# Two group-normalized convolutions on one core: alternating rows, 32x64 products, one straight step on TensorE

## The chip, the cores and the metric

The kernel runs on one core of a Trainium2 chip. The time is device time in microseconds (us) for one execution. The core's engines are named as in the profile: PE is TensorE (PEld its loads of weights), DVE is VectorE, ACT is ScalarE, POOL is GpSimd, SP is SyncE, which only issues transfers (DMAs). Each runs its own program in order; they meet at semaphores. PSUM has eight banks of 128 partitions x 512 float32, into which TensorE alone adds up.

## The reference

```
def _gn(v, G=16, eps=1e-05):          # group norm: 16 groups of 2 channels
    ...
    return ((g - m) / jnp.sqrt(s + eps)).reshape(v.shape)

x = x + _L0_conv_ref(_gn(x), L0_conv_weight, L0_conv_threshold)   # 3x3, weights masked by a threshold
x = x + _L1_conv_ref(_gn(x), L1_conv_kernel, L1_conv_bias)        # 5x5, with bias
```

x has 16 images of 32 channels, 128 x 128, float32. Both convolutions keep the size. The second needs the mean and the variance of the whole image that the first has made.

## The kernel before, in words

**Tiling.** An image is worked in two halves, so there are 32 halves, h. The 128 partitions are four quads of 32 channels. For reading, quad i holds a band of rows with its halo (`x_bands`, 18 rows, six slots; `mid_bands`, 20 rows, three slots). For results, quad j of bank i holds the j-th part of band i: `mid` (five slots) and `x_own` (two slots) have four rows of 128 in each bank. A weight matrix of one tap is 32x32, so quad i of the image times tap t gives quad j of bank i for four rows: one product of 32 x 32 cells and 512 columns. 16 of them, for all i and j, are a set (`tap`, L784), and fill the array.

**Precision.** Image and weights are each the sum of two float16 values. A convolution is three passes: high image x high weights, high image x low weights, low image x high weights. The 3x3 has 9 sets per pass, the 5x5 25; together 102 sets per step.

**Steps.** Step s does the 3x3 convolution of half s and the 5x5 of half s - 3 (`LAG`). TensorE has a loop of bodies between which it branches (`first3`, `inner3`, `last3`, `first5`, `inner5`, `last5`, `low_image`, L796 to L861): the body of the 3x3 taps is run three times, with `s3` overwritten in between by ScalarE (`weights3`) and `x3` overwritten in place by VectorE with the low image (`low3`); the 5x5 body twice, with `s5` overwritten by ScalarE (`weights5`). Three lead steps have 3x3 alone, three last steps 5x5 alone.

**The other engines, in a step.** ScalarE empties the 5x5 banks (`take_conv5`), copies weights, takes roots, and writes the high images (`high3` for half s + 1, `high5` for half s - 2). VectorE writes the low images (`low5`, `low3`), normalizes in place (`normalize3`, `normalize5`, L597), makes `mid` from the 3x3 banks and `x_own` (`take_conv3`, which releases the banks through `bank3_go`), and takes statistics (`stats_in`, `stats_out`, `aggregate`). GpSimd adds the 5x5 result to `mid`. Once per image the statistics go over DRAM to all partitions (`spread_stats`, `gather_stats` on ScalarE's queue); VectorE sums them (`group_stats`), ScalarE takes the root, VectorE refines it (`scale_of`). In even steps from 4 to 28 there are two such statistics, one of `mid`, one of x.

**Transfers.** SyncE issues, in an order written out by hand: `load_bands`, `load_own`, `move_mid` (16 per half, from `mid` to `mid_bands`), `move_edges` (the rows that cross halves, 14 per image) and `store_out`.

Of the kernel before, what the change touches and what calls it, by code (L numbers as in the profile page):

```python
# [48 lines left out]
def two_blocks(nc, x, w3_dram, thr_dram, w5_dram, bias_dram, mix_dram, out):  # L49
# [7 lines left out]
    with ExitStack() as ctx:  # L57
# [14 lines left out]
        x3 = sbuf("x3", [P, R3, PITCH], F16)  # L72
# [18 lines left out]
        carrier = sbuf("carrier", [P, 2])  # L91
# [52 lines left out]
        c3_early = sem("c3_early")  # L144
        c3_inner = sem("c3_inner")
        c3_whole = sem("c3_whole")
        a5_inner = sem("a5_inner")
        a5_whole = sem("a5_whole")
        b5_whole = sem("b5_whole")
# [7 lines left out]

        hi5_done = sem("hi5_done")
        conv5_out = sem("conv5_out")
# [41 lines left out]
        MOVES = Q * Q + 2 * Q - 1  # L201
        CLEARED = 3 + XB_SLOTS + 2 * MB_SLOTS
# [4 lines left out]
        def own_rows(image, r, j):  # L207

            return image.rearrange("c (i r j a) w -> r j c i (a w)", i=BANKS, r=2, j=Q)[r, j]

        def band(r, i, halo):

            first = A * Q * (2 * i + r) - halo
# [9 lines left out]
        def _(sp):  # L223
            def load_own(h):
                for j in range(Q):
                    sp.dma_start(x_own[quad(j), h % X_SLOTS, :, :], own_rows(x[h // 2], h % 2, j),
                                 ).then_inc(x_own_in[h % X_SLOTS], 16)

            def store_out(k, banks):
                for j in range(Q):  # L230
                    sp.dma_start(own_rows(out[k // 2], k % 2, j)[:, banks, :], mid[quad(j), k % MID_SLOTS, banks, :],
                                 ).then_inc(out_stored[k % MID_SLOTS], 16)
# [7 lines left out]
            def move_rows(h, i, j, k, to, rows, at):  # L240

                sp.dma_start(mid_bands[quad(to), k % MB_SLOTS, at:at + rows.stop - rows.start, :],  # L242
                             mid[quad(j), h % MID_SLOTS, i, :].rearrange("p (a w) -> p a w", a=A)[:, rows, :],
                             ).then_inc(mid_bands_in[k % MB_SLOTS], 16)

            def move_mid(h):
                sp.wait_ge(mid_made, PIECES * (h + 1))
                for i in range(Q):
                    for j in range(Q):
                        move_rows(h, i, j, h, i, slice(0, A), 2 + A * j)  # L250

            def move_edges(n, source, to):

                sp.wait_ge(mid_made, PIECES * (2 * n + source + 1))
                for i in range(Q):
                    if source < to:
                        move_rows(2 * n, i, Q - 1, 2 * n + 1, i, slice(A - 2, A), 0)
                        if i:
                            move_rows(2 * n, i, 0, 2 * n + 1, i - 1, slice(0, 2), 2 + A * Q)
                    else:  # L260
                        move_rows(2 * n + 1, i, 0, 2 * n, i, slice(0, 2), 2 + A * Q)
                        if i + 1 < Q:
                            move_rows(2 * n + 1, i, Q - 1, 2 * n, i + 1, slice(A - 2, A), 0)
# [28 lines left out]
            for s in range(LAG, STEPS + 1):  # L292
# [10 lines left out]
                if has3(s + XB_SLOTS):  # L303
                    sp.wait_ge(norm1, s + 2)
# [12 lines left out]
        def _(pool):  # L317
            for t in (x3, x5_hi, x5_lo):
                nc.gpsimd.memset(t[:, :, 0:2], 0.0)
                nc.gpsimd.memset(t[:, :, PITCH - 2:PITCH], 0.0).then_inc(zeroed, 1)  # L320
            cleared = 3
# [18 lines left out]
            nc.gpsimd.tensor_copy(s5[:, :, :], s5_hi[:, :, :]).then_inc(w5_go, 1)  # L340
# [3 lines left out]
            for i in range(Q):  # L344
                for j in range(Q):
                    pool.dma_start(mid_bands[quad(i), 1, 2 + A * j:2 + A * (j + 1), :],
                                   mid[quad(j), 1, i, :].rearrange("p (a w) -> p a w", a=A),
                                   ).then_inc(mid1_moved, 16)
# [12 lines left out]
        def _(act):  # L361
# [6 lines left out]
            def high3(h):  # L368

                act.wait_ge(norm1, h + 1)  # L370
                if h:
                    act.wait_ge(c3_whole, 2 * h)
                nc.scalar.activation(x3[:, :, 2:2 + W], x_bands[:, h % XB_SLOTS, :, :], ACT.Copy).then_inc(x3_go, 2)  # L373

            def high5(k):

                act.wait_ge(norm2, k + 1)
                if k:
                    act.wait_ge(a5_whole, k)
                nc.scalar.activation(x5_hi[:, :, 2:2 + W], mid_bands[:, k % MB_SLOTS, :, :], ACT.Copy).then_inc(hi5_done, 1)  # L380

# [7 lines left out]

            def weights3(source, part, tokens):  # L390

                at, go = ((slice(0, 4), w3a_go), (slice(4, T3), w3b_go))[part]
                nc.scalar.activation(s3[:, at, :], source[:, at, :], ACT.Copy).then_inc(go, tokens)  # L393

            def weights5(source):
                nc.scalar.activation(s5[:, :, :], source[:, :, :], ACT.Copy).then_inc(w5_go, 1)  # L396
# [590 lines left out]
```

## Time and profile before

| | us |
|---|---|
| median of three runs | 855.02 (852.67 to 856.11) |
| the profiled execution | 854.08 |
| its span | 852.3 |
| TensorE busy (92%) | 780.7 |
| VectorE busy (81%) | 692.6 |
| ScalarE busy (38%) | 319.7 |
| GpSimd busy (38%) | 322.4 |
| mean TensorE clock | 0.983 of full |

The share of a busy engine is an average over stretches with different limits, so the rows further below take the span apart: by stretch, then one step, then the single instructions. In a row of the timeline the first number is the start in us from the span's start, the second the duration; `xN` is the number of instructions merged in it, and the bracket at its end is the idle time of that engine before it and what ended that. "issue" means that the profile shows nothing that was waited for.

### The profile page before, as it was taken

How to read it: one execution, taken by the hardware profiler on the slowest of the kernel's cores; microseconds unless marked ns; L12 is line 12 of the kernel's file. 1: busy time of each engine (PE TensorE's matmuls, PEld its weight loads, DVE VectorE, ACT ScalarE, POOL GpSimd, SP SyncE). 2: the span in 40 equal slices, each digit the busy share in tenths (PEclk: the TensorE clock that was granted, in tenths of full speed). 3: DMA queues.
4: the chain of work that ended last, by engine and by line, in shares of the span. 5: the costliest groups of instructions: out<-in, count | busy, mean ns of one | idle time of the engine just before them, and what ended most of it. 6: DMA issues, size and time to landing. Idle time of an engine off the chain costs nothing.

```text
span 852.3 us, 108960 instructions
## 1 busy us (share of the span) xinstructions
PE 780.7 (92%) x52277; PEld 694.1 (81%) x52277; DVE 692.6 (81%) x1008; ACT 319.7 (38%) x408; POOL 322.4 (38%) x164
## 2 busy tenths in 40 slices
PE   0874689999999999999999999999999999998995
PEld 0553579888989889889988989988998989987884
DVE  6877599899897989799898989899897968675432
ACT  0312134443443434443443434444343434443221
POOL 1035043333434443233444444333344444333331
PEclk9997799999999999999999999999999999999998
DMA  8999638788695968788685978878695737563413
GB/s 179 222 219 234 149 83 212 197 207 206 178 223 139 224 171 212 193 211 203 173 220 139 225 180 212 198 198 212 171 228 139 205 95 189 121 167 80 103 49 99
DMA packets 83778, 150.51 MB, mean 177 GB/s; under 512 B 21152, under 2 KB 28576, under 8 KB 79648
## 3 DMA queue, kind: packets, MB, share of 16 engines
q1 hardware_dynamic: 78624, 144.88, 69.0%
q10 hardware_dynamic: 4608, 4.23, 2.2%
q0 software_dynamic: 512, 1.05, 0.5%
q14 instruction: 25, 0.20, 0.1%
q8 instruction: 9, 0.15, 0.1%
HBM read 75.60 MB, written 33.59 MB: 128 GB/s over the span
## 4 chain that ended last, share of the span: by engine, by line
PE 78%; DVE 11%; issue 4%; DMA 3%; SPq 2%; DVEq 1%; ACT 1%; ACTq 0%; POOLq 0%; POOL 0%
PE psum L790 78%; DVE x L620 3%; SPq L242 2%; DMA mid_bands<-mid 1%; DMA x_bands<-x_dram 1%; DVE x_bands L605 1%; DVE bn_in L543 1%; DVEq L643 1%; DVE bn_out L648 1%; DVE mid_bands L605 1%; DVE mid L640 1%; DVE product L575 0%; DVE x_lo L628 0%; DVE deviation L579 0%; DVE gscale L594 0%
## 5 line engine op out<-in xcount | busy, mean ns | idle before, releaser
L354 POOL TENSOR_TENSOR mid<-mid,conv_out 128x512 f32<-128x512 f32 x122 | 300.4, 2492 | 471.9 <-ACT conv_out L387 471.9
L790 PE MATMUL psum<-x_hi,s 32*32 32x512 f16 x25600 | 373.1, 378 | 17.8 <-issue 10.3
L790 PEld LDWEIGHTS psum<-x_hi,s 32*32 32x32 f16 x25600 | 339.7, 88 | 42.1 <-issue 17.2
L790 PE MATMUL psum<-x,s 32*32 32x512 f16 x13824 | 225.3, 386 | 19.4 <-DVEq L643 12.0
L790 PEld LDWEIGHTS psum<-x,s 32*32 32x32 f16 x13824 | 174.8, 88 | 70.1 <-issue 40.1
L790 PE MATMUL psum<-x_lo,s_hi 32*32 32x512 f16 x12800 | 186.4, 376 | 3.2 <-issue 3.2
L790 PEld LDWEIGHTS psum<-x_lo,s_hi 32*32 32x32 f16 x12800 | 176.4, 88 | 8.3 <-issue 5.0
L628 DVE TENSOR_TENSOR x_lo<-mid_bands,x_hi 128x2560 f16<-128x2560 f32 x32 | 103.9, 3247 | 33.6 <-PE psum L790 31.6
L620 DVE TENSOR_TENSOR x<-x_bands,x 128x2304 f16<-128x2304 f32 x32 | 101.3, 3166 | 36.3 <-PE psum L790 36.3
L387 ACT ACTIVATE conv_out<-psum,bias,unscale 128x512 f32<-128x512 f32 x122 | 90.4, 769 | 61.1 <-PE psum L790 58.3
L396 ACT ACTIVATE s<-s_lo 128x800 f16<-128x800 f16 x29 | 25.3, 871 | 158.1 <-PE psum L790 158.1
L373 ACT ACTIVATE x<-x_bands 128x2304 f16<-128x2304 f32 x32 | 67.9, 2122 | 38.8 <-DVE x_bands L613 23.0
L640 DVE SCALAR_TENSOR_TENSOR mid<-psum,unscale,x_own 128x1024 f32<-128x1024 f32 x64 | 79.1, 1277 | 3.8 <-PE psum L790 2.8
L648 DVE BATCH_NORM_STATS2 bn_out<-mid 128x6 f32<-128x512 f32 x128 | 78.0, 668 | 2.2
L543 DVE BATCH_NORM_STATS2 bn_in<-x_bands 128x6 f32<-128x512 f32 x128 | 78.2, 673 | 1.3 <-DMA x_bands<-x_dram 1.0
L380 ACT ACTIVATE x_hi<-mid_bands 128x2560 f16<-128x2560 f32 x32 | 74.4, 2326 | 2.9 <-DVE mid_bands L613 2.9
L396 ACT ACTIVATE s<-s_hi 128x800 f16<-128x800 f16 x32 | 27.9, 872 | 124.3 <-PE psum L790 124.3
L605 DVE TENSOR_SCALAR x_bands<-x_bands,gmean,gscale 128x2304 f32<-128x2304 f32 x32 | 71.7, 2242 | 0.1
L605 DVE TENSOR_SCALAR mid_bands<-mid_bands,gmean,gscale 128x2560 f32<-128x2560 f32 x32 | 51.6, 1612 | 2.7 <-DMA mid_bands<-mid 0.6
L366 ACT ACTIVATE root<-gvar 128x1 f32<-128x1 f32 x32 | 6.5, 202 | 79.3 <-DVE gvar L583 53.3
L393 ACT ACTIVATE s<-s_lo 128x128 f16<-128x128 f16 x64 | 20.6, 322 | 33.9 <-PE psum L790 33.8
L393 ACT ACTIVATE s<-s_hi 128x128 f16<-128x128 f16 x64 | 17.2, 315 | 25.7 <-PE psum L790 25.7
(80 smaller groups left out, 196.5 us busy)
## 6 DMA issues: line engine op xcount, KB each, us to landing
x_own<-x_dram SPq DMA_DIRECT2D x128, 256.0 KB
mid_bands<-mid SPq DMA_DIRECT2D x496, 64.0 KB
out_dram<-mid SPq DMA_DIRECT2D x116, 256.0 KB
x_bands<-x_dram SPq DMA_DIRECT2D x96, 288.0 KB
x_bands<-x_dram SPq DMA_DIRECT2D x32, 272.0 KB
mid_bands<-mid SPq DMA_DIRECT2D x224, 32.0 KB
every_mv<-mv_scratch ACTq DMA_DIRECT2D x16, 256.0 KB, 3.7
out_dram<-mid SPq DMA_DIRECT2D x24, 128.0 KB
```

The costliest lines, as they stand in the source:

```text
L354: nc.gpsimd.tensor_tensor(m, m, conv_out[:, b, :], ALU.add).then_inc(out_added, 1)
L373: nc.scalar.activation(x3[:, :, 2:2 + W], x_bands[:, h % XB_SLOTS, :, :], ACT.Copy).then_inc(x3_go, 2)
L380: nc.scalar.activation(x5_hi[:, :, 2:2 + W], mid_bands[:, k % MB_SLOTS, :, :], ACT.Copy).then_inc(hi5_done, 1)
L387: nc.scalar.activation(conv_out[:, b, :], psum[:, X5_BANK + b, :], ACT.Identity, bias=bias[:, 0:1], scale=unscale[:, 1:2]).then_inc(conv5_ ...
L396: nc.scalar.activation(s5[:, :, :], source[:, :, :], ACT.Copy).then_inc(w5_go, 1)
L543: nc.vector.bn_stats(bn_in[:, h // 2 % 2, h % 2, b, :], rows.rearrange("p a w -> p (a w)")).then_inc(bn_x, 1)
L605: nc.vector.tensor_scalar(v, v, gmean[:, which:which + 1], gscale[:, which:which + 1], ALU.subtract, ALU.mult).then_inc(scaled, 1)
L620: nc.vector.tensor_tensor(at, x_bands[:, h % XB_SLOTS, :, :], at, ALU.subtract).then_inc(x3_go, 1)
L628: nc.vector.tensor_tensor(x5_lo[:, :, 2:2 + W], mid_bands[:, k % MB_SLOTS, :, :], x5_hi[:, :, 2:2 + W], ALU.subtract).then_inc(b5_go, 1)
L640: nc.vector.scalar_tensor_tensor(mid[:, h % MID_SLOTS, at, :], psum[:, X3_BANK + at.start:X3_BANK + at.stop, :], unscale[:, 0:1], x_own[:, ...
L648: nc.vector.bn_stats(bn_out[:, h % 2, b, :], mid[:, h % MID_SLOTS, b, :]).then_inc(bn_mid, 1)
L790: ins = nc.tensor.matmul(psum[quad(j), bank + i, :].rearrange("p (a w) -> p a w", a=A), w[quad(i), at, :], src[quad(i), A * j + dy:A * (j ...
```

## The change

**Rows.** Half h is now 64 rows in one piece, and quad j holds every fourth row (r = 4m + j). Each row of 128 is a piece of its own in the transfers of `x_own`, `mid` and the results. `piece` gives the rows that go from quad j of `mid` to band i, mostly five. Only two rows cross from one half to the other: `move_edges` has two transfers each way.

```
 def own_rows(image, r, j):
-    return image.rearrange("c (i r j a) w -> r j c i (a w)", i=BANKS, r=2, j=Q)[r, j]
+    return image.rearrange("c (r i m j) w -> r j c (i m) w", r=2, i=BANKS, j=Q)[r, j]
...
+def piece(h, i, j):
+    first = A * i - (1 if j >= 2 and i else 0)
+    last = A * (i + 1) + (1 if j < 2 and i + 1 < BANKS else 0)
+    top = 2 + j + A * (first - A * i)
+    return (mid_bands[quad(i), h % MB_SLOTS, top:top + A * (last - first - 1) + 1:A, :],
+            as_rows(mid, j, h % MID_SLOTS)[:, first:last, :])
```

**Products.** Neighbouring rows j and j + 1 need the same image row with taps dy and dy - 1, so one product of 32 x 64 cells does both (`pairs`). The taps that are left over are 32x32 (`singles`). High and low parts of image and weights have buffers of their own (`x3_hi`, `x3_lo`; `s3`, `s5` are gone), and TensorE's step is one straight body; the last three steps have a second one.

```
+def pairs(w, src, k, bank, start=False, every=None):
+    for dx in range(k):
+        x0 = 2 - k // 2 + dx
+        for dy in range(1, k):
+            at = dx * k + k - 1 - dy
+            for i in range(Q):
+                for J in range(2):
+                    top = 2 * J + dy
+                    ins = nc.tensor.matmul(
+                        psum[2 * C * J:2 * C * (J + 1), bank + i, :].rearrange("p (a w) -> p a w", a=A),
+                        w[quad(i), at:at + 2, :].rearrange("p t o -> p (t o)"),
+                        src[quad(i), top:top + A * (A - 1) + 1:A, x0:x0 + W], ...
...
+with nc.body("whole_step", valid_engines=only):
+    hint = pe.mark_branch_hint_location()
+    high_image3()
+    high_image5()
+    low_image3()
+    low_image5(step)
+    pe.br_lt(step, HALVES, on_true="whole_step", on_false="before_last").branch_hint(hint)
+with nc.body("before_last", valid_engines=only):
+    pe.br("last_steps")
+with nc.body("last_steps", valid_engines=only):
+    high_image5()
+    low_image5(step)
+    pe.br_lt(step, STEPS, on_true="last_steps", on_false="all_done")
```

`high_image3` is pairs, then singles, each with high and low weights; `high_image5` singles, then pairs; `low_image3` pairs, singles; `low_image5` singles (then `b5_begun`), pairs. `c3_whole` comes after `low_image3`.

**Normalization.** ScalarE does it, as an activation with scale `gscale` and bias `nbias`, in place, and clears the pad rows by copying zeros. VectorE does the first half only (`first_normalize3`), and computes `nbias` at the end of each `scale_of`.

```
+def normalize3(h):
+    act.wait_ge(scale_known, ROOTS.index(("x", h // 2)) + 1)
+    act.wait_ge(x_bands_in[h % XB_SLOTS], 16 * Q * (h // XB_SLOTS + 1))
+    act.wait_ge(bn_x, BANKS * (h + 1))
+    scale_by(0, x_bands[:, h % XB_SLOTS, :, :])
...
 def high3(h):
     act.wait_ge(norm1, h + 1)
     if h:
-        act.wait_ge(c3_whole, 2 * h)
+        act.wait_ge(c3_whole, h)
```

**VectorE's step** loses both normalizations, and its later part is in another order:

```
     if gathered:
         dve.wait_ge(mv_in, 16 * exchange_number(s - 1))
         group_stats(gathered[0])
         scale_of(gathered[0])
+    if len(gathered) > 1:
+        group_stats(gathered[1])
+    if has3(s + 5):
+        stats_in(s + 5, range(BANKS))
+    if len(gathered) > 1:
+        dve.wait_ge(norm1, s + 2)
+        scale_of(gathered[1])
     if has3(s):
         take_conv3(s)
...
-    if len(gathered) > 1:
-        group_stats(gathered[1])
-    if has3(s + 5):
-        stats_in(s + 5, range(BANKS))
-    if len(gathered) > 1:
-        scale_of(gathered[1])
```

The order of instructions shows three places. First TensorE's loop, before, from its head on (L790 is a product of `tap`):

```order
L790 MATMUL psum<-x,s 32x512 x16
L935 UNCONDITIONAL_BRANCH
L790 MATMUL psum<-x,s 32x512 x32
L812 REGISTER_ALU
L790 MATMUL psum<-x,s 32x512 x96
L938 COMPARE_AND_BRANCH
L790 MATMUL psum<-x,s 32x512 x16
L941 COMPARE_AND_BRANCH
L790 MATMUL psum<-x_hi,s 32x512 x16
L944 UNCONDITIONAL_BRANCH
```

and the whole loop of the changed kernel (L777 is a pair product, 64 output partitions, L795 a single one):

```order
L777 MATMUL psum<-x_hi,s_hi 64x512 x48
L777 MATMUL psum<-x_hi,s_lo 64x512 x48
L795 MATMUL psum<-x_hi,s_hi 32x512 x48
L795 MATMUL psum<-x_hi,s_lo 32x512 x48
L795 MATMUL psum<-x_hi,s_hi 32x512 x80
L795 MATMUL psum<-x_hi,s_lo 32x512 x80
L777 MATMUL psum<-x_hi,s_hi 64x512 x160
L777 MATMUL psum<-x_hi,s_lo 64x512 x160
L777 MATMUL psum<-x_lo,s_hi 64x512 x48
L795 MATMUL psum<-x_lo,s_hi 32x512 x128
L828 REGISTER_ALU
L777 MATMUL psum<-x_lo,s_hi 64x512 x160
```

The branches between the parts are gone; between 64 and 32 output partitions the loop changes four times, its own end included.

Second, ScalarE in an even step, before, from `gather_stats` on (`x_hi<-mid_bands` is `high5`, `x<-x_bands` is `high3`):

```order
L408 DMA every_mv<-mv_scratch 128x512 [waits mv_out]
L396 ACTIVATE s<-s_lo 128x800 [waits a5_inner]
L366 ACTIVATE root<-gvar 128x1 [waits var_ready]
L373 ACTIVATE x<-x_bands 128x18x128 [waits c3_whole,norm1]
L396 ACTIVATE s<-s_hi 128x800 [waits a5_whole]
L380 ACTIVATE x_hi<-mid_bands 128x20x128 [waits a5_whole,norm2]
L366 ACTIVATE root<-gvar 128x1 [waits var_ready]
```

and after:

```order
L437 DMA every_mv<-mv_scratch 128x512 [waits mv_out]
L394 ACTIVATE x_bands<-x_bands,nbias,gscale 128x2304 [waits bn_x,x_bands_in1,scale_known]
L404 ACTIVATE x_bands<-zeros 32x128 [waits act_scaled]
L372 ACTIVATE root<-gvar 128x1 [waits var_ready]
L394 ACTIVATE mid_bands<-mid_bands,nbias,gscale 128x2560 [waits mid_bands_in1,scale_known]
L416 ACTIVATE mid_bands<-zeros 32x256 [waits act_scaled]
L379 ACTIVATE x_hi<-x_bands 128x18x128 [waits c3_whole,norm1]
L387 ACTIVATE x_hi<-mid_bands 128x20x128 [waits b5_begun,norm2]
L372 ACTIVATE root<-gvar 128x1 [waits var_ready]
```

The weight copies are gone, the two normalizations stand ahead of `high3`, and the second root still stands behind `high5`.

Third, VectorE in an even step, after, from the end of the second `group_stats` on (`mid<-psum` is `take_conv3`):

```order
L605 SCALAR_TENSOR_TENSOR gvar<-sums 128x1 [waits gstep]
L565 BN_STATS bn_in<-x_bands 128x6 [waits x_bands_in1]
L565 BN_STATS bn_in<-x_bands 128x6 x3
L612 RECIPROCAL rinv<-root 128x1 [waits root_ready,norm1]
L613 TENSOR_TENSOR newton<-gvar,rinv 128x1 [waits gstep]
L614 TENSOR_TENSOR newton<-newton,rinv 128x1 [waits gstep]
L615 TENSOR_SCALAR newton<-newton 128x1 [waits gstep]
L616 SCALAR_TENSOR_TENSOR gscale<-rinv,newton 128x1 [waits gstep]
L618 SCALAR_TENSOR_TENSOR nbias<-gmean,gscale 128x1 [waits gstep]
L657 SCALAR_TENSOR_TENSOR mid<-psum,unscale,x_own 128x1024 [waits c3_whole,x_own_in0,out_stored4]
```

Before, `take_conv3` of the same step stood behind the first `scale_of`, and the second statistic behind it:

```order
L594 SCALAR_TENSOR_TENSOR gscale<-rinv,newton 128x1 [waits gstep]
L640 SCALAR_TENSOR_TENSOR mid<-psum,unscale,x_own 128x1024 [waits x_own_in0,c3_whole,out_stored4,gstep]
L640 SCALAR_TENSOR_TENSOR mid<-psum,unscale,x_own 128x1024
L605 TENSOR_SCALAR mid_bands<-mid_bands,gmean,gscale 128x2560 [waits mid_bands_in0]
L613 MEMSET mid_bands 32x256 [waits scaled]
L648 BN_STATS bn_out<-mid 128x6 [waits mid_made] x4
L575 SCALAR_TENSOR_TENSOR product,sums<-every_mv,mix 128x128
```

So `take_conv3` has moved behind the second `scale_of`.

**SyncE.** `load_own(0)` stands ahead of the w5 loads, bands 5 to 7 come later among the first transfers, and a band's slot is refilled after `low3` instead of after the normalization.

## Rows read from the trace of the kernel before

**Rows 1.** Busy time by stretch: start:end, length, busy per engine, clock, DMA share, GB/s

```profile
0.00:71.56 71.56, 35.24 (x1349) 22.77 (x1349) 55.45 (x125) 16.16 (x21) 18.35 (x35) 0.94 0.99 209
71.56:115.50 43.94, 30.78 (x1632) 24.17 (x1632) 30.84 (x52) 7.38 (x9) 3.65 (x8) 0.83 0.68 156
115.50:784.20 668.70, 663.32 (x45696) 599.86 (x45696) 581.28 (x804) 281.77 (x362) 279.80 (x112) 1.00 0.73 184
784.20:852.30 68.10, 51.39 (x3629) 47.32 (x3603) 25.07 (x29) 14.41 (x16) 20.57 (x10) 0.97 0.32 83
```

**Rows 2.** Timeline of TensorE's weight loads over one step: start, duration, what, idle before

```profile
403.37 2.11 PEld L790 LDWEIGHTS psum<-x,s 32*32 32x32 f16 x144 [0.35 <-issue]
405.74 0.23 PEld L790 LDWEIGHTS psum<-x,s 32*32 32x32 f16 x32 [0.26 <-issue]
...
415.68 5.49 PEld L790 LDWEIGHTS psum<-x_hi,s 32*32 32x32 f16 x400 [0.17 <-issue]
421.09 5.57 PEld L790 LDWEIGHTS psum<-x_lo,s_hi 32*32 32x32 f16 x400
427.01 0.57 PEld L790 LDWEIGHTS psum<-x,s 32*32 32x32 f16 x39 [0.35 <-issue]
```

**Rows 3.** TensorE's products: two of the timeline, one group of the page

```profile
32.22 1.89 PE L878 MATMUL psum<-warm 128*128 128x512 f16 x8
...
421.25 5.72 PE L790 MATMUL psum<-x_lo,s_hi 32*32 32x512 f16 x400
...
L790 PE MATMUL psum<-x_lo,s_hi 32*32 32x512 f16 x12800 | 186.4, 376 | 3.2 <-issue 3.2
```

**Rows 4.** Timeline of ScalarE: root, high3, high5, and four banks emptied

```profile
416.39 0.20 ACT L366 ACTIVATE root<-gvar 128x1 f32<-128x1 f32 x1 [1.85 <-DVE gvar L583]
416.50 2.11 ACT L373 ACTIVATE x<-x_bands 128x2304 f16<-128x2304 f32 x1
...
422.35 2.33 ACT L380 ACTIVATE x_hi<-mid_bands 128x2560 f16<-128x2560 f32 x1
...
784.60 2.79 ACT L387 ACTIVATE conv_out<-psum,bias,unscale 128x512 f32<-128x512 f32 x4 [2.38 <-PE psum L790]
```

**Rows 5.** Timeline: take_conv3 (mid) and TensorE behind it; VectorE's refined root

```profile
37.00 2.48 DVE L640 SCALAR_TENSOR_TENSOR mid<-psum,unscale,x_own 128x1024 f32<-128x1024 f32 x2
...
39.67 0.66 PE L790 MATMUL psum<-x,s 32*32 32x512 f16 x32 [1.43 <-DVEq L643]
...
416.62 0.17 DVE L590 RECIPROCAL rinv<-root 128x1 f32<-128x1 f32 x1 [0.27 <-ACT root L366]
...
417.59 2.47 DVE L640 SCALAR_TENSOR_TENSOR mid<-psum,unscale,x_own 128x1024 f32<-128x1024 f32 x2
```

**Rows 6.** Timeline of the lead: TensorE's first set, GpSimd's split of w5

```profile
27.27 4.60 PE L790 MATMUL psum<-x,s 32*32 32x512 f16 x288 [0.28 <-ACT x L373]
...
56.74 2.29 POOL L336 TENSOR_SCALAR w<-w,wfac 128x800 f32<-128x800 f32 x1 [51.86 <-DVE carrier L712]
...
59.09 3.22 POOL L338 CAST s_hi<-w 128x800 f16<-128x800 f32 x1
...
64.20 1.70 POOL L341 TENSOR_TENSOR s_lo<-w,s_hi 128x800 f16<-128x800 f32 x1
```

**Rows 7.** Timeline of TensorE's weight loads: the first loop pass, then the end

```profile
81.65 1.77 PEld L790 LDWEIGHTS psum<-x_hi,s 32*32 32x32 f16 x128 [2.41 <-issue]
...
95.52 0.21 PEld L790 LDWEIGHTS psum<-x_hi,s 32*32 32x32 f16 x32 [6.11 <-issue]
...
787.47 5.44 PEld L790 LDWEIGHTS psum<-x_hi,s 32*32 32x32 f16 x400 [3.24 <-ACTq L432]
793.70 5.50 PEld L790 LDWEIGHTS psum<-x_hi,s 32*32 32x32 f16 x400 [0.78 <-DVE s L749]
```

**Rows 8.** SyncE's issues of moved rows (timeline); the page's queue 1: packets, MB, share

```profile
402.69 13.94 SPq L242 DMA_DIRECT2D mid_bands<-mid  x22
...
q1 hardware_dynamic: 78624, 144.88, 69.0%
```

More of the change, by code:

```diff
@@ L230, in store_out @@
                 for j in range(Q):
-                    sp.dma_start(own_rows(out[k // 2], k % 2, j)[:, banks, :], mid[quad(j), k % MID_SLOTS, banks, :],
-                                 ).then_inc(out_stored[k % MID_SLOTS], 16)
+                    sp.dma_start(own_rows(out[k // 2], k % 2, j)[:, A * banks.start:A * banks.stop, :],
+                                 as_rows(mid, j, k % MID_SLOTS, banks)).then_inc(out_stored[k % MID_SLOTS], 16)
             def load_bands(h):
@@ L431, in _ @@
                 if has5(s):
[L432 to L436 removed]
+                    act.drain().then_inc(x5_hi_go, 1)
                 if s == LAG:
@@ new lines, in singles @@
+            def singles(w, src, k, bank, start=False):
+                for dx in range(k):
+                    x0 = 2 - k // 2 + dx
+                    for i in range(Q):
+                        for j in range(Q):
+                            dy = 0 if j % 2 == 0 else k - 1
+                            at = dx * k + k - 1 - dy
+                            ins = nc.tensor.matmul(
+                                psum[quad(j), bank + i, :].rearrange("p (a w) -> p a w", a=A), w[quad(i), at, :],
+                                src[quad(i), j + dy:j + dy + A * (A - 1) + 1:A, x0:x0 + W],
+                                start=start and dx == 0, stop=True, skip_group_check=True, tile_position=(i * C, j * C))
+                return ins
@@ new lines, in high_image3, with low_image3 @@
+            def high_image3():
+                pe.wait_ge(bank3_go, 1)
+                pe.wait_ge(x3_hi_go, 1)
+                pairs(s3_hi, x3_hi, K3, X3_BANK, start=True, every=x3_hi_go)
+                pairs(s3_lo, x3_hi, K3, X3_BANK, every=bank3_go)
+                singles(s3_hi, x3_hi, K3, X3_BANK)
+                singles(s3_lo, x3_hi, K3, X3_BANK)
+            def low_image3():
+                pe.wait_ge(x3_lo_go, 1)
+                pairs(s3_hi, x3_lo, K3, X3_BANK, every=x3_lo_go)
+                singles(s3_hi, x3_lo, K3, X3_BANK).then_inc(c3_whole, 1)
@@ new lines, in high_image5, with low_image5 @@
+            def high_image5():
+                pe.wait_ge(x5_hi_go, 1)
+                singles(s5_hi, x5_hi, K5, X5_BANK, start=True)
+                singles(s5_lo, x5_hi, K5, X5_BANK)
+                pairs(s5_hi, x5_hi, K5, X5_BANK, every=x5_hi_go)
+                pairs(s5_lo, x5_hi, K5, X5_BANK).then_inc(a5_whole, 1)
+            def low_image5(step):
+                pe.wait_ge(x5_lo_go, 1)
+                singles(s5_hi, x5_lo, K5, X5_BANK).then_inc(b5_begun, 1)
+                pe.reg_add(step, step, 1)
+                pairs(s5_hi, x5_lo, K5, X5_BANK, every=x5_lo_go).then_inc(b5_whole, 1)
@@ L956, in _ @@
-            with nc.body("past", valid_engines=only):
-                pe.reg_add(visit5, visit5, ALONE)
-                pe.br_lt(step, STEPS, on_true="first5", on_false="all_done")
+                high_image3()
+                high_image5()
+                low_image3()
+                low_image5(step)
+                pe.br_lt(step, HALVES, on_true="whole_step", on_false="before_last").branch_hint(hint)
+            with nc.body("before_last", valid_engines=only):
+                pe.br("last_steps")
```

430 lines of the change are left out of this document (154 added, 276 removed).

## The prediction, made before the changed kernel ran

> **What bounds the kernel now.** I read first the busy time by stretch [rows 1]. It cuts the span into the lead (71.6 us), the first pass of TensorE's loop with both convolutions (43.9), 28 further steps (668.7, or 23.88 each) and the end (68.1, with the last three steps). In the 28 steps TensorE is busy for 99% of the time at full clock; VectorE has 581 of 669 us, ScalarE 282. Then one step, by the rows of TensorE's weight loads [rows 2]: it begins at 403.37 and the next at 427.01, 23.64 us. A step has 102 sets of 16 products of 32x32, since 16 of them fill the array. 25 sets lie between 415.68 and 421.09: 0.217 us each. A product lasts 0.376 us on average, longer than the pace, since the next set starts while it drains. A single product of 128x128 with 512 columns has the same pace: eight in 1.89 us, so (1.89 - 0.38)/7 = 0.216 [rows 3]. The array bounds the sets; 102 of them are 22.1 us. The other 1.5 us of a step is idle time where TensorE goes from one body of its program to the next or meets a wait between them: 0.35 at the loop's end, 0.26 and 0.17 at two of the others, put down to "issue" [rows 2]. Nobody is waited for there. So the middle of the kernel can lose at most 1.5 us a step, some 42 us in all, unless a new wait comes.
>
> **TensorE's straight step.** A pair product covers two output rows' taps in 32x64 cells, so 8 pair products fill the array for one set's time, and the 3x3 needs 3x2 sets of pairs and 3 of singles per pass, the 5x5 5x4 and 5: again 9 and 25. 102 sets stay 102, at 0.217: nothing is gained by the form itself. Of the boundaries only the loop's own stays: 22.1 + 0.35 = 22.5 us. New is that the array goes from 32x64 to 32x32 tiles or back four times a step. No row shows that. From below it costs 0, as the gaps of today may already hold whatever a change costs; from above 0.17, if the next form must wait until a product is through (0.38 against the pace of 0.217 [rows 3]). I take 0.1, in the middle. The Trainium skill (TensorEngine Tiling (Array Packing), Key Properties) says that changing the tiling mode drains TensorE; no row here tests it. By it the upper end would hold and the forecast rise by some 7 us.
>
> **The chain of even steps.** This term decides. In 13 of the 28 steps (even s from 4 to 28) VectorE now does `scale_of` of the second statistic before `take_conv3(s)`, and waits for its root. ScalarE issues that root behind `high3(s+1)` and `high5`, and `high3(s+1)` waits for the step's whole 3x3 convolution, because it overwrites the image that TensorE reads. TensorE may not begin the next step before `take_conv3` has emptied its banks. From the last 3x3 set to the next step it is: 0.34 until the products are through and ScalarE starts (25 sets from 421.25 end nominally at 426.68, the row at 426.97; 0.05 for the signal) [rows 3]; 2.11 high3, 2.33 high5, 0.20 root [rows 4]; 0.1 and 0.05 for drain and start between them (four copies end at 787.39, TensorE goes on at 787.47 [rows 4, 7]); 0.03 to VectorE, 0.97 for its five small steps (416.62 to 417.59), 0.2 for the added `nbias`, one more such step; 2.47 for take_conv3; 0.19 from its end at 39.48 to TensorE at 39.67 [rows 5]. Together 9.0 us. Beside it TensorE has 25 low sets and the loop, 5.8 us. So it stands still for 3.2 us. An even step is 77 sets (16.7) + 9.0 + three changes of tiles (0.3) = 26.0 us; every other step 22.5 + 0.4 = 22.9. Now that wait does not exist: take_conv3 is right behind the step's first `scale_of`, 9.4 us ahead of the next step [rows 2, 5].
> 13 x 26.0 + 15 x 22.9 = 681.5. Today's 28 steps take 6.8 us more than 28 x 23.64; of such irregular waits I keep 4. So 685.5 against 668.7: **+16.8**. With changes of tiles at no cost +7, at 0.17 +24.
>
> **The engines beside it.** VectorE loses both normalizations and TensorE's weight copies go from ScalarE; ScalarE gets two passes like high3 and high5 (2.11 and 2.33 [rows 4]) and two short clears, for about 5 us more and 3 less. Around 12 us of 23 hides, except where its order counts, as above. In other steps ScalarE empties four banks in 2.79 us [rows 4] + 0.4 for ends and drain, while TensorE has 18 sets (3.9): no wait, but 0.7 us of slack, and on odd steps ScalarE first waits for VectorE's statistics.
>
> **Transfers.** Own rows, results and moved rows now lie in pieces of one row (512 B) instead of four. Queue 1 moved 144.88 MB in 78624 packets and had the engines for 69.0% of the span [rows 8]: 120 ns each, 1.84 KB on average, 15.4 B/ns. 512 B would take 33 ns if the time goes by bytes. Under load a byte is dearer: the lead moved 209 GB/s at a share of 0.99, the middle 184 at 0.73 [rows 1], a fifth apart. I allow a third: 44. About 6600 such pieces a step (2048 in, 2048 out, 2432 moved) are 13.6 to 18.1 us of 16 engines, the bands' 1.15 MB 4.7, the rest 0.5: 19 to 23 us, below the mean step of 24.3. SyncE issues 30 transfers a step instead of 35 (edges fall from 14 to 4 in two steps), at 13.94/22 = 0.63 us each [rows 8]: 19 us. Both hide, so I charge nothing; the cover is thin.
>
> **The lead.** First product to loop: 27.27 to 71.56, 44.3 us [rows 1, 6]. After: step 0 is 27 sets (5.9) + 0.34 + 2.47 + 0.19 = 8.9, since the low image has its own buffer. Step 1 adds about 2 for normalization and copy, 10.9. Step 2 ends when GpSimd has split w5 (2.3 + 3.2 + 1.7 [rows 6], the copy between them gone), which VectorE releases some 8.5 us into it: 16. Sum 36, or -8.3. The extra `nbias` and a colder clock in the idle times take some back: **-7.5** (bounds -4 and -9).
>
> **Code seen the first time.** In the first pass TensorE stops after each 128 products or so: five times, from about 2 us up to 6.11 (2.41 the first [rows 7]). No engine is the releaser, so I read them as waits for code. The new loop has 1008 products against 976 in the old bodies, with no repeats between: I take **+3** (-8 to +8). And the last three steps have a body of their own (720 products): five new stops, in lighter traffic 1.8 each, 9; the one at its head hides behind ScalarE. The trace says stops; the Trainium skill (Runtime: NRT & Kernel Launch, Instruction fetch mechanics) says that a sequential crossing of a block is mostly hidden. By it both terms would be about zero and the time some 17 us less; here the trace shows the stops in straight 5x5 code.
>
> **The end.** Three stops for VectorE's weight copy (0.78 [rows 7]) go: -2.4. Changes of tiles +0.6, smaller stores +0.5, code +9: **+7.7**.
>
> Sum against the profiled span: 852.3 + 16.8 - 7.5 + 3 + 7.7 = 872.3. The profiled run took 854.1, 1.8 over its span, and the median is 855.0; with 1.8 I forecast **874 us**.
>
> **Rivals.**
> Code is there in time (-12), tile changes are free (-10), or both: 874 - 22 = 852; 848 to 862. For it: straight code. Against: the stops of rows 7. 0.18.
> Transfers become the bound: at 50 ns a piece a step needs 25.7 us of engine time, 28 steps 720 instead of 685.5: 909; 886 to 915. It decides above 46 ns. For it: a share of 0.99 at 209 GB/s in the lead [rows 1]. Against: the 0.73 of the middle. 0.13.
> **Faster:** TensorE's set is bound by its 32 instructions, not the array. A pair set has half, and 78 of 102 sets are pairs. At 0.19 a pair set, odd steps lose 2.1 us and even ones 1.6: 13 x 1.6 + 15 x 2.1 = 52, so 822; it decides as soon as a pair set takes under 0.205. Against it stands the 0.216 of the full product, two instructions [rows 3]. With what I may have read wrong in the chain (without the 3.2 us the sum is 832) 0.15.
> The loop of some 2020 instructions doesn't stay loaded, so the straight step is no gain: one stop of 2.4 a step, 940. The old one, just smaller, stays. 0.04.
> My forecast, 862 to 886: 0.50.
>
> **The numbers.** 843 to 896 leaves out most of the fast rival, the loop that reloads and half of the transfers' case. About 0.5% is what a measurement tells from no change: faster by more than that (below 850.7) 0.18, within 0.11, slower 0.71.
>
> **What would show it.** TensorE's loads in straight runs of 22.5 to 23 us; before every second step of the middle an idle time near 3 us ended by VectorE's drain behind take_conv3, and `rinv` waiting for ScalarE's root. Gaps of about 0.1 at the four changes. Stops of 2 us every 128 products in the first loop pass and the first of the last steps. Wrong: a pair set below 0.205; take_conv3 ended before the low 5x5; a DMA share near 1 with VectorE waiting for stored results.

## The result, and the profile after

| | us |
|---|---|
| median before (four runs) | 854.75 (852.67 to 856.11) |
| median after (four runs) | 906.54 (905.56 to 907.94) |
| ratio | 1.061 (1.058 to 1.064) |
| forecast | 874, range 843 to 896 |
| profiled execution, its span | 905.56, 903.7 |

The direction was right and the size wrong: 52 us slower where 19 were forecast, outside the range. The busy time by stretch of the kernel after, cut at the same events as [rows 1] (start:end, length, busy time of PE, PEld, DVE, ACT, POOL, clock, DMA share, GB/s):

```profile
0.00:68.55 68.55, 35.52 (x910) 18.71 (x911) 48.32 (x115) 18.23 (x14) 9.28 (x28) 0.93 0.93 190
68.55:117.89 49.34, 34.98 (x1006) 18.57 (x1008) 23.69 (x42) 15.38 (x10) 8.46 (x16) 0.71 0.86 178
117.89:829.80 711.91, 672.37 (x28229) 444.33 (x28224) 473.31 (x728) 356.48 (x304) 196.94 (x112) 0.97 0.74 173
829.80:903.70 73.90, 55.16 (x2176) 31.98 (x2160) 23.21 (x25) 17.89 (x17) 20.07 (x10) 0.95 0.33 79
```

Beside [rows 1]: lead -3.0, first pass +5.4, the 28 steps +43.2, end +5.8. TensorE was busy for 99% of the middle and is now for 94%, and the clock of the middle, 1.00 before, is 0.97. TensorE's weight loads where an even step ends and over the following one (start, duration, what, idle before):

```profile
751.25 4.12 PEld L777 LDWEIGHTS psum<-x_lo,s_hi 32*64 32x64 f16 x160 [0.24 <-issue]
758.82 0.45 PEld L777 LDWEIGHTS psum<-x_hi,s_hi 32*64 32x64 f16 x24 [3.45 <-DVEq L660]
759.48 0.22 PEld L777 LDWEIGHTS psum<-x_hi,s_hi 32*64 32x64 f16 x8 [0.21 <-issue]
759.91 0.22 PEld L777 LDWEIGHTS psum<-x_hi,s_hi 32*64 32x64 f16 x8 [0.21 <-issue]
...
763.26 0.63 PEld L795 LDWEIGHTS psum<-x_hi,s_hi 32*32 32x32 f16 x48 [0.42 <-issue]
763.81 0.74 PEld L795 LDWEIGHTS psum<-x_hi,s_lo 32*32 32x32 f16 x48
...
783.48 1.22 PEld L777 LDWEIGHTS psum<-x_hi,s_hi 32*64 32x64 f16 x48
```

Two things are to be seen. TensorE's loads stop for 3.45 us, ended by L660, the drain behind `take_conv3`. Then sets start 0.43 apart (759.48, 759.91), twice the usual 0.217: these rows of 8 are one set each. The granted clock says the same, 0.61 of full on average in the first 4.4 us of that step and 1.00 in the rest of it (the last number but two):

```profile
758.80:763.20 4.40, 4.37 (x96) 2.17 (x96) 4.34 (x5) 4.27 (x3) 2.95 (x3) 0.61 0.37 86
763.20:783.48 20.28, 20.28 (x917) 13.81 (x913) 8.65 (x8) 5.64 (x4) 0.00 (x0) 1.00 0.63 148
```

Within 0.3 us of its first product TensorE was at 1.2 GHz, and it was back at 2.4 GHz some 4 us after the wait. And the chain that made the wait, on ScalarE and VectorE in the same even step:

```profile
746.86 0.16 DVE L605 SCALAR_TENSOR_TENSOR gvar<-sums 128x1 f32<-128x1 f32 x1
755.16 0.16 DVE L612 RECIPROCAL rinv<-root 128x1 f32<-128x1 f32 x1 [8.15 <-ACT root L372]
...
756.25 2.48 DVE L657 SCALAR_TENSOR_TENSOR mid<-psum,unscale,x_own 128x1024 f32<-128x1024 f32 x2
...
750.34 2.13 ACT L379 ACTIVATE x_hi<-x_bands 128x2304 f16<-128x2304 f32 x1 [2.23 <-PE psum L795]
752.63 2.34 ACT L387 ACTIVATE x_hi<-mid_bands 128x2560 f16<-128x2560 f32 x1 [0.17 <-issue]
754.88 0.19 ACT L372 ACTIVATE root<-gvar 128x1 f32<-128x1 f32 x1
```

VectorE had the variance ready at 747.0 and stood still for 8.15 us for a root of 0.2 us that was queued behind `high3` and `high5`; `high3` itself began only at 750.34, after 2.23 us of waiting for TensorE's 3x3 products. In [rows 5] nothing of the kind stood ahead of `take_conv3`.

### The profile page after: what moved, and what is told of

The parts are those of the page before. It is cut to its first block, busy times and chain, and to the rows that moved or that the text cites. A ratio compares the mean times of both kernels' runs of the same rounds, so it can differ in the third digit from the quotient of the medians.

```text
span 903.7 us, 67842 instructions
## 1 busy us (share of the span) xinstructions
PE 798.0 (88%) x32302; PEld 513.6 (57%) x32302; DVE 568.5 (63%) x907; ACT 408.0 (45%) x345; POOL 234.7 (26%) x165
## 3 DMA queue, kind: packets, MB, share of 16 engines
q1 hardware_dynamic: 228768, 144.67, 70.0%
q0 software_dynamic: 704, 1.25, 0.6%
## 4 chain that ended last, share of the span: by engine, by line
PE 76%; issue 7%; DVE 6%; ACT 4%; DVEq 2%; DMA 1%; ACTq 1%; POOL 1%; SPq 1%; POOLq 0%
PE psum L777 57%; PE psum L795 19%; ACT x_hi L379 3%; DVE mid L657 2%; DVEq L660 2%; DMA x_bands<-x_dram 1%; DVE bn_out L665 1%; DVE bn_in L565 1%; ACTq L455 1%; ACT conv_out L424 0%; SPq L251 0%; ACT root L372 0%; DVE x_lo L636 0%; DVE rinv L612 0%; DVE newton L613 0%
## 5 line engine op out<-in xcount | busy, mean ns | idle before, releaser
L360 POOL TENSOR_TENSOR mid<-mid,conv_out 128x512 f32<-128x512 f32 x122 | 217.0, 1808 | 604.2 <-ACT conv_out L424 604.2
L777 PE MATMUL psum<-x_hi,s_hi 32*64 32x512 f16 x6656 | 216.3, 405 | 47.4 <-DVEq L660 40.4
L777 PE MATMUL psum<-x_hi,s_lo 32*64 32x512 f16 x6656 | 204.7, 388 | 5.1 <-issue 5.1
L777 PE MATMUL psum<-x_lo,s_hi 32*64 32x512 f16 x6656 | 201.3, 381 | 3.1 <-issue 3.1
L777 PEld LDWEIGHTS psum<-x_hi,s_hi 32*64 32x64 f16 x6656 | 110.1, 109 | 138.6 <-DVEq L660 47.3
L777 PEld LDWEIGHTS psum<-x_hi,s_lo 32*64 32x64 f16 x6656 | 127.3, 108 | 73.6 <-issue 18.8
L777 PEld LDWEIGHTS psum<-x_lo,s_hi 32*64 32x64 f16 x6656 | 113.3, 104 | 75.0 <-issue 14.4
L636 DVE TENSOR_TENSOR x_lo<-x_bands,x_hi 128x2304 f16<-128x2304 f32 x32 | 97.9, 3060 | 0.0
L795 PE MATMUL psum<-x_hi,s_hi 32*32 32x512 f16 x4096 | 76.9, 388 | 14.4 <-issue 7.3
L394 ACT ACTIVATE mid_bands<-mid_bands,nbias,gscale 128x2560 f32<-128x2560 f32 x32 | 80.5, 2517 | 19.9 <-DVE nbias L618 19.5
L795 PE MATMUL psum<-x_hi,s_lo 32*32 32x512 f16 x4096 | 78.2, 388 | 0.7 <-issue 0.7
L795 PEld LDWEIGHTS psum<-x_hi,s_hi 32*32 32x32 f16 x4096 | 52.9, 88 | 36.2 <-issue 22.4
L795 PE MATMUL psum<-x_lo,s_hi 32*32 32x512 f16 x4096 | 66.6, 380 | 1.1 <-issue 1.1
L795 PEld LDWEIGHTS psum<-x_hi,s_lo 32*32 32x32 f16 x4096 | 61.9, 88 | 3.8 <-issue 1.6
```

Of the source, the lines that this page charges most:

```text
L360: nc.gpsimd.tensor_tensor(m, m, conv_out[:, b, :], ALU.add).then_inc(out_added, 1)
L394: nc.scalar.activation(v, v, ACT.Identity, bias=nbias[:, at], scale=gscale[:, at]).then_inc(act_scaled, 1)
L636: nc.vector.tensor_tensor(x3_lo[:, :, 2:2 + W], x_bands[:, h % XB_SLOTS, :, :], x3_hi[:, :, 2:2 + W], ALU.subtract).then_inc(low3_done, 1)
L777: ins = nc.tensor.matmul(psum[2 * C * J:2 * C * (J + 1), bank + i, :].rearrange("p (a w) -> p a w", a=A), w[quad(i), at:at + 2, :].rearran ...
L795: ins = nc.tensor.matmul(psum[quad(j), bank + i, :].rearrange("p (a w) -> p a w", a=A), w[quad(i), at, :], src[quad(i), j + dy:j + dy + A ...
```

## The experiments

The first experiment and the one with two changes of tiles were timed four times, every other one once. The kernel before was timed again beside each group: 859.2 us beside the first four runs, 858.1 and 859.4 beside the later ones, where the result's table has 854.8, so a difference of 5 us between groups says nothing.

Step lengths below are from TensorE's first product of a step to that of the next. In the kernel after, the 13 even steps (4 to 28) average 26.44 us, the 13 odd ones behind them 24.77, and step 30, where no such wait is, has 23.17. Differences in time are to 906.5 unless said.

**Put take_conv3 first again.** One part of the change undone:

```
-                if len(gathered) > 1:
-                    dve.wait_ge(norm1, s + 2)
-                    scale_of(gathered[1])
                 if has3(s):
                     take_conv3(s)
                     stats_out(s)
+                if len(gathered) > 1:
+                    dve.wait_ge(norm1, s + 2)
+                    scale_of(gathered[1])
```

> The changed kernel with one part undone: in even steps VectorE does take_conv3 and stats_out before the second scale_of, as in the kernel before; nothing else differs. Theory (the wait of TensorE for take_conv3 at the end of even steps, 3.35 us, and the half clock of the 8 or 9 sets behind it, 1.5 us, are what made the middle long): both vanish in 13 steps, every step is 23.16 us like the clean ones of the changed kernel, 906.5 - 13 x (3.35 + 1.5) = 843 us, below the 855 of the kernel before. Rival (transfers in 512 B pieces hold the middle at its pace, 886 to 915 as forecast for that case): the wait only moves to another place, the time stays at 895 to 906. Rival (the clock falls for another reason than the wait): 13 x 1.5 stays, 863.

Measured: 843.9 us, ratio to the kernel before 0.986 (0.980 to 0.993). Of the middle, and of VectorE in an even step:

```profile
116.06:766.00 649.94, 649.27 (x28212) 436.75 (x28208) 482.49 (x728) 356.69 (x304) 257.77 (x112) 1.00 0.83 189
```

```profile
413.44 2.48 DVE L657 SCALAR_TENSOR_TENSOR mid<-psum,unscale,x_own 128x1024 f32<-128x1024 f32 x2 [1.11 <-PE psum L795]
416.06 2.47 DVE L665 BATCH_NORM_STATS2 bn_out<-mid 128x6 f32<-128x512 f32 x4
418.44 0.15 DVE L612 RECIPROCAL rinv<-root 128x1 f32<-128x1 f32 x1
```

TensorE is busy for all of the 649.9 us, at clock 1.00; the first of these steps has 24.4 us, the others 23.1 to 23.4. VectorE takes up the root with no idle time ahead of it. So the order of two calls on VectorE cost 62.6 us (62.0 of them in the middle, 711.9 against 649.9) and turned a gain of 1.4% into a loss of 6%. The rival with the transfers as the bound falls: with the wait gone they simply ran denser, 0.83 of the time instead of 0.74.

**Two shorter waits.** The root between `high3` and `high5` (first cut), and on top of that 1.25 us of statistics between the second `scale_of` and `take_conv3` (second cut):

```
                     if has3(s + 1):
                         high3(s + 1)
+                    if len(gathered) > 1:
+                        take_root(gathered[1])
                     if has5(s + 1):
                         high5(s + 1 - LAG)
-                if len(gathered) > 1:
-                    take_root(gathered[1])
```

> The changed kernel with ScalarE's second root between high3 and high5 instead of behind high5; VectorE's order is left as changed. The chain that ends in take_conv3 is shorter by high5 and the start behind it, 2.34 + 0.17 us, so TensorE's wait should fall from 3.35 to about 0.85 us. If the clock falls after any wait: 906.5 - 13 x 2.5 = 874 us and half clock behind each wait. If it takes a longer wait for that: 906.5 - 13 x (2.5 + 1.5) = 854.5. If transfers are the bound, 895 to 906.

```
                 if has3(s + 5):
-                    stats_in(s + 5, range(BANKS))
+                    stats_in(s + 5, range(2 if len(gathered) > 1 else BANKS))
                 if len(gathered) > 1:
                     dve.wait_ge(norm1, s + 2)
                     scale_of(gathered[1])
+                    if has3(s + 5):
+                        stats_in(s + 5, range(2, BANKS))
```

> As the run with the root between high3 and high5, but two of the four statistics of x (1.25 us) stand between the second scale_of and take_conv3. TensorE's wait should be 0.85 + 1.25 = 2.1 us, between the two others, to see at which wait the clock falls. Full clock kept: 906.5 - 13 x (1.25 + 1.5) = 871 us. Clock lost as in the changed kernel: 906.5 - 13 x 1.25 = 890.

Measured: 855.6 and 871.6, each the value for a full clock. One such row behind the wait, of the first and of the second kernel (its lines are numbered two higher), and the clock of the second behind it:

```profile
333.80 1.04 PEld L777 LDWEIGHTS psum<-x_hi,s_hi 32*64 32x64 f16 x48 [1.17 <-DVEq L660]
```

```profile
340.21 1.04 PEld L779 LDWEIGHTS psum<-x_hi,s_hi 32*64 32x64 f16 x48 [2.31 <-DVEq L660]
```

```profile
340.20:344.60 4.40, 4.39 (x217) 2.89 (x218) 4.36 (x5) 4.18 (x5) 4.40 (x4) 1.00 0.37 86
```

All 48 loads, six sets, are in one row of 1.04 us, and 217 products start in 4.4 us where the kernel after started 96. From the second kernel to the one after the time went up by 35 us. The 13 waits add up to 29.2 us in the one and 45.2 in the other, so 16 of it is the waits themselves and the other 19 the clock.

The length of a wait does not tell alone what the clock does. In the second kernel 11 waits have 2.31 us and the last 1.17, all with full clock behind them, but the first has 2.65, and behind it the clock fell. In the kernel after it fell behind 12 of the 13 waits; behind the one that ended at 197.9, of 3.45 us like the others, it stayed. The kernel before has both too, a clock of 0.61 behind a stop of 3.06 us and 1.00 behind the 3.24 us of [rows 7]:

```profile
144.63 0.18 PEld L779 LDWEIGHTS psum<-x_hi,s_hi 32*64 32x64 f16 x16 [2.65 <-DVEq L660]
144.60:149.00 4.40, 4.37 (x96) 2.07 (x96) 4.34 (x5) 4.17 (x5) 4.40 (x4) 0.61 0.37 86
```

```profile
197.90:202.30 4.40, 4.38 (x215) 2.86 (x217) 4.35 (x5) 4.27 (x3) 2.95 (x3) 1.00 0.33 78
```

```profile
86.40:90.80 4.40, 3.63 (x128) 2.41 (x127) 2.27 (x4) 0.00 (x0) 0.00 (x0) 0.61 1.10 233
787.40:791.80 4.40, 4.33 (x320) 4.15 (x321) 0.12 (x1) 0.00 (x0) 4.40 (x4) 1.00 0.66 162
```

What else decides was not tried.

**The kernel before with the new order alone.** Second statistic and its `scale_of` ahead of `take_conv3` and `stats_out`:

```
+                if has5(s + 1) and not s % 2:
+                    normalize5(s + 1 - LAG)
+                if len(gathered) > 1:
+                    group_stats(gathered[1])
+                if has3(s + 5):
+                    stats_in(s + 5, range(BANKS))
+                if len(gathered) > 1:
+                    scale_of(gathered[1])
                 if has3(s):
                     take_conv3(s)
-                if has5(s + 1) and not s % 2:
-                    normalize5(s + 1 - LAG)
...
```

> The kernel before with the new order alone: VectorE does the second statistic and its scale_of before take_conv3 and stats_out (normalize5 stays ahead, since high5 needs it). By the trace of before the second root can be done at 424.95, scale_of at 426.0, take_conv3 at 428.5 where TensorE now goes on at 427.01: a wait of 1.65 us, and 1.3 us for the low image of the next step behind the statistics. 13 x 2.95 = +38, about 893 us, and up to 10 more if the clock falls after it. If this order costs nothing by itself, 855.

Measured: 875.7 us, 16.5 over the kernel before as timed beside it; the span is 873.8, 21.5 over that of [rows 1]. VectorE and TensorE at the end of an even step:

```profile
288.66 0.16 DVE L590 RECIPROCAL rinv<-root 128x1 f32<-128x1 f32 x1 [1.30 <-ACT root L366]
...
289.62 2.48 DVE L640 SCALAR_TENSOR_TENSOR mid<-psum,unscale,x_own 128x1024 f32<-128x1024 f32 x2
```

```profile
292.26 2.07 PEld L789 LDWEIGHTS psum<-x,s 32*32 32x32 f16 x144 [1.76 <-issue]
```

The wait is 1.76 - 0.33 (what stands at that place in its odd steps), times 13: 18.6 of the 21.5. The 893 of the expectation was a miss: TensorE waited for the low 3x3 image for 2.8 us in the whole run, where it had waited 4.7 in the kernel before, so the later low image held it up no more. The same order costs here about a third of what it costs in the changed kernel: the wait is shorter, and the granted clock of the 4.4 us behind it is 1.00.

**Changes of tiles, two fewer and two more.** Both on top of the first experiment. Fewer (TensorE's products alone: their waits and the step counter are left out, and the lines stand in a helper of their own; VectorE makes `low3(s + 1)` right behind `take_conv3(s)`):

```
                 high_image3()
-                high_image5()
-                low_image3()
-                low_image5(step)
+                singles(s5_hi, x5_hi, K5, X5_BANK, start=True)
+                singles(s5_lo, x5_hi, K5, X5_BANK)
+                singles(s5_hi, x5_lo, K5, X5_BANK)
+                singles(s3_hi, x3_lo, K3, X3_BANK)
+                pairs(s3_hi, x3_lo, K3, X3_BANK, every=x3_lo_go).then_inc(c3_whole, 1)
+                pairs(s5_hi, x5_hi, K5, X5_BANK, every=x5_hi_go)
+                pairs(s5_lo, x5_hi, K5, X5_BANK).then_inc(b5_begun, 1)
+                pairs(s5_hi, x5_lo, K5, X5_BANK, every=x5_lo_go).then_inc(b5_whole, 1)
```

> On top of a1_conv_first, TensorE's loop takes its products in another order, so that it goes between 32x64 and 32x32 tiles twice a step instead of four times (all 32x32 products stand together), with c3_whole already after 42 of the 102 sets, and VectorE makes the low 3x3 image of the next half in the step before. Theory: a clean step takes 23.16 us, 102 sets of 0.217 are 22.13, so each change costs (23.16 - 22.13) / 4 = 0.26 us; two fewer in 29 passes give -15: 829 us. If the 1.03 us has another cause (the loop itself, group starts), the time stays at 843.

More:

```
                 singles(s5_hi, x5_hi, K5, X5_BANK, start=True)
+                pairs(s5_hi, x5_hi, K5, X5_BANK, every=x5_hi_go)
                 singles(s5_lo, x5_hi, K5, X5_BANK)
-                pairs(s5_hi, x5_hi, K5, X5_BANK, every=x5_hi_go)
```

> On top of a1_conv_first, high_image5 takes singles, pairs, singles, pairs instead of singles, singles, pairs, pairs: six changes of tiles a step instead of four, and as many more in the last three. By 0.26 us each: + 2 x 0.26 x 32 = +17, about 861 us. If changes cost nothing, 844.

Measured: 834.6 us with two changes, ratio to the kernel before 0.972 (0.969 to 0.976); 854.4 with six. By step: 22.82 us with two, 23.18 with four, 23.51 with six: 0.17 us a change. The rows show it with two changes first, six below:

```profile
149.00 1.83 PEld L797 LDWEIGHTS psum<-x_lo,s_hi 32*32 32x32 f16 x128
151.07 1.04 PEld L779 LDWEIGHTS psum<-x_lo,s_hi 32*64 32x64 f16 x48 [0.24 <-issue]
152.21 4.31 PEld L779 LDWEIGHTS psum<-x_hi,s_hi 32*64 32x64 f16 x160
```

```profile
172.48 4.12 PEld L777 LDWEIGHTS psum<-x_hi,s_hi 32*64 32x64 f16 x160 [0.24 <-issue]
177.02 1.06 PEld L795 LDWEIGHTS psum<-x_hi,s_lo 32*32 32x32 f16 x80 [0.42 <-issue]
178.31 4.12 PEld L777 LDWEIGHTS psum<-x_hi,s_lo 32*64 32x64 f16 x160 [0.23 <-issue]
```

Wherever the shape changes the loads pause for 0.24 or 0.42 us, and between parts of the same shape these rows show no pause; part of a pause is the lead that loads have over products. The expected 0.26 a change was too high, since it put all of the 1.03 us over 102 sets on the changes. Some 0.35 us over 102 sets of 0.217 remain in every variant; no rows tell what they are.

**Is it the straight code?** The step cut into four bodies joined by unconditional branches:

```
                 high_image3()
+                pe.br("step_high5")
+            with nc.body("step_high5", valid_engines=only):
                 high_image5()
...
```

> a1_conv_first with the straight step cut into four bodies joined by three unconditional branches, at the places between high_image3, high_image5, low_image3 and low_image5. If a boundary costs what the rows of the kernel before show (0.17 to 0.35 us): 28 x 3 x 0.2 = +17, about 861 us, and the straight code is worth that much. If a branch alone costs nothing: 844.

Measured: 842.8 us. The place of one of the three branches, between high and low images:

```profile
407.68 4.33 PEld L777 LDWEIGHTS psum<-x_hi,s_lo 32*64 32x64 f16 x160
412.04 1.28 PEld L777 LDWEIGHTS psum<-x_lo,s_hi 32*64 32x64 f16 x48
```

No idle time stands at it, and the steps have 23.2 us as in the first experiment. So an unconditional branch between bodies that stay loaded costs nothing here, and the 0.17 to 0.35 us of [rows 2] belonged to something else at those places (conditional branches, compares on counters, waits for weights or images overwritten in place); which, was not tried.

**Is it the 32x64 form?** Each pair product written as two of 32x32 cells, in all places or in one or two of the 5x5's passes. The sets and sums are the same; TensorE's loop has 1632, 1328 or 1168 products instead of 1008:

```
-                            for J in range(2):
-                                top = 2 * J + dy
+                            for j in range(Q):
+                                top = 2 * (j // 2) + dy
...
-                                    w[quad(i), at:at + 2, :].rearrange("p t o -> p (t o)"),
+                                    w[quad(i), at + j % 2, :],
...
-                                    tile_position=(i * C, 2 * C * J))
+                                    tile_position=(i * C, j * C))
```

> a1_conv_first with every 32x64 product written as two of 32x32 cells: the same 102 sets and the same sums, no change of tiles, 1632 products instead of 1008 in the loop. If the set is bound by the array and the longer loop stays loaded: 22.13 us a step instead of 23.16, so 844 - 29 = 815 us, which would mean that the 32x64 form brought nothing. If the loop is too long to stay loaded, stops as in its first pass (2 to 6 us each 128 products or so) in every step: 25 us or more a step longer, above 1400.

> On top of a1_conv_first, only the pairs of the 5x5's high image by low weights are written as 32x32 products: 1168 products in TensorE's loop instead of 1008, the same sets. With every pair split (1632 products) the loop reloaded its code in each pass and took 1775 us; this run and the next ask how far the changed kernel's loop is from that. The loop stays loaded: 844 us. If reloading begins as soon as the loop is longer than what stays, a few stops of some 2 us in each of 29 passes: from 960 us up.

> As the run before it, with the pairs of the high image by high weights split too: 1328 products in the loop. The loop stays loaded: 844 us. If the code that stays is replaced in turn, every part of a loop that is somewhat too long is gone when it comes round again: 11 stops of 2.3 us each pass, about 1500 us.

Measured: 1774.9, 1404.2 and 1509.7 us. A step of the 1168-product loop, and two of the stops in the step before it:

```profile
427.80:470.55 42.75, 28.97 (x1168) 17.44 (x1168) 14.80 (x15) 13.08 (x11) 9.95 (x5) 0.93 0.45 107
```

```profile
409.28 2.58 PEld L796 LDWEIGHTS psum<-x_hi,s_lo 32*32 32x32 f16 x128 [4.47 <-issue]
413.05 1.03 PEld L796 LDWEIGHTS psum<-x_hi,s_lo 32*32 32x32 f16 x66 [1.18 <-issue]
```

With 16% more products the loop stops eight or nine times in a pass, in all its parts and mostly 128 products apart, and a step takes 42.75 us instead of 23.18. No releaser is shown at these stops; that they are the code being loaded again is read from their spacing and from their coming with the length alone. In these runs the value of the 32x64 form lies here: its sets are no faster (20 sets from 771.22 to 775.58 in the kernel after, 0.218 each), but with 1008 products instead of 1632 the straight step stays loaded. The kernel before did not need that, as it ran its bodies two and three times. The Trainium skill (Runtime: NRT & Kernel Launch, Instruction fetch mechanics) gives TensorE room for 2048 instructions, refilled in blocks of 256 in order; the runs agree: 1008 products with their loads are 2016 and stay, 1168 are 2336 and don't, and 128 products with their loads are a block. Its sentence that crossing a block is mostly hidden does not hold here: in new code most crossings show a stop, of 0.4 to 6.0 us in the kernel after, and only some show none.

## Why the prediction was wrong, point by point

The terms, against the profiled span: forecast 872.3, measured 903.7, 31.4 more.

| | forecast | measured |
|---|---|---|
| lead | -7.5 | -3.0 |
| first pass | +3 | +5.4 |
| 28 steps | +16.8 | +43.2 |
| end | +7.7 | +5.8 |

**The chain of even steps** was right in place, cause and count, and nearly in size: a wait of 3.2 us forecast, 3.45 between loads measured, in steps 4 to 28, ended by the drain behind `take_conv3`. Undoing it gave back all.

**What failed is the step behind it.** The sum took the odd step after each wait at 22.9 us, as if TensorE would go on at 2.4 GHz. In 12 of the 13 it ran on at 1.2 GHz first, and those 13 steps had 24.77 us on average, 1.6 over the clean 23.18: 20.7 us, two thirds of the whole miss. The rows had it to be seen: [rows 1] has the clock at 0.83 in the first pass, where TensorE had long stops [rows 7], but the prediction allowed for "a colder clock" in the lead alone. The shorter waits show that it was no matter of course: behind 2.31 us the clock stayed.

**Changes of tiles** cost 0.17 us each, the upper bound; 0.1, "in the middle", was too low, 6.9 us over the 28 steps. That upper bound was what followed if a product must be through before the next shape starts, and the Trainium skill (TensorEngine Tiling (Array Packing), Key Properties) says just that, that changing the mode drains TensorE; the measured 0.17 us agrees, though no run shows the draining itself. With 0.17 the clean step comes to 22.5 + 0.68 = 23.18, as measured.

**The allowance** of 4 us for irregular waits hid a part: even steps took another 3.0 over the forecast. 20.7 + 6.9 + 3.0 - 4 = 26.6 of the 26.4 us by which the middle missed.

**The lead** gained 3.0 instead of 8.3 or 7.5. Step 0 was to take 8.9 us and took 13.6 (28.70 to 42.29). In it TensorE stopped for 2.61 us, which I read as the wait for new code, since nobody releases it, and went on at half clock:

```profile
33.03 0.12 PEld L777 LDWEIGHTS psum<-x_lo,s_hi 32*64 32x64 f16 x7 [0.23 <-issue]
35.76 0.20 PEld L777 LDWEIGHTS psum<-x_lo,s_hi 32*64 32x64 f16 x15 [2.61 <-issue]
36.14 0.24 PEld L777 LDWEIGHTS psum<-x_lo,s_hi 32*64 32x64 f16 x8 [0.19 <-issue]
36.57 0.24 PEld L777 LDWEIGHTS psum<-x_lo,s_hi 32*64 32x64 f16 x8 [0.19 <-issue]
```

The prediction counted such stops in the first loop pass and the end, and none in the lead. Its steps 1 and 2 were near (11.4 and 14.9 us for 10.9 and 16), and the first product came 1.4 us later than in [rows 6].

**First pass and end** were right in kind: five stops of 1.05 to 5.99 us, and in the first of the last steps five of 0.45 to 1.43, 4.8 in sum, where 1.8 each were taken. One of each:

```profile
84.80 0.16 PEld L795 LDWEIGHTS psum<-x_hi,s_hi 32*32 32x32 f16 x18 [5.99 <-issue]
```

```profile
837.84 0.16 PEld L795 LDWEIGHTS psum<-x_hi,s_lo 32*32 32x32 f16 x20 [1.41 <-issue]
```

**Transfers** stayed a cover, as forecast: 19.3 us of a step of 23.2 (0.83, first experiment), within the 19 to 23 of the sum. Queue 1 of the page, where [rows 8] had 78624 packets:

```profile
q1 hardware_dynamic: 228768, 144.67, 70.0%
```

That is 0.700 x 903.7 x 16 / 228768 = 44 ns for 632 B, or 14.3 B/ns against 15.4 before: a third as long per packet, and a byte 8% dearer, not a third. Their limit was not tested.

**The rivals.** "Faster, as pair sets are not bound by the array" falls: 0.218. "Free tile changes" falls, and so does "code in time", which the prediction priced at 17 us in one place and at 12 in the other (its two terms, 3 and 9, are 12). The rival of transfers gave 886 to 915 and so held the measured time, by a mechanism that is not there: a time inside a rival's range is no evidence for it. The rival that the loop doesn't stay loaded was 16% of products away, and priced far too low: one stop of 2.4 us a step, 940 us, where the loop of 1168 products stops eight or nine times and took 1404.

## What to carry to other kernels

On an in-order engine, ask of every wait what is queued behind it: what releases the bounding engine belongs ahead of anything that waits for a third engine's late work. Price also what such a wait does behind itself: here the clock made a wait of 3.45 us cost about 5. And ask first whether a long loop body stays loaded; fewer, larger products can be worth more for that than for their own speed.

## What the runs showed of the hardware

- Behind idle times of its loads of 1.17 and 2.31 us in the loop TensorE went on at 2.4 GHz every time. Behind the 13 waits of 3.45 us (the first 3.77) it ran at 1.2 GHz for 7 to 9 sets, some 4 us, 11 times, once longer and once not at all. Single stops of 2.61 and 2.65 us had 1.2 GHz behind them, one of 3.24 us 2.4 GHz, so length alone does not decide.
- A change between 32x64 and 32x32 tiles costs 0.17 us; unconditional branches between loaded bodies cost nothing measurable (842.8 against 843.9 us).
- A loop of 1008 products ran without stops; one of 1168 stopped mostly every 128 products in every pass: 1404 against 844 us for the same arithmetic.
- The fastest kernel of this study, 834.6 us, is the changed one with `take_conv3` first and all 32x32 products of a step together.
